# Second attention of a two-layer kernel: denominator, output and value units spread one or two to a batch, maxima spread after the next maxima, another order at the loop's end

## The reference, cut to what matters

```python
def _L1_attn_ref(x, gamma, w_qkv, w_out):
    ...
    xn = rms_norm(x, gamma)
    qkv = xn @ w_qkv
    ...
    q = q * scale
    sim = jnp.einsum('bhid,bhjd->bhij', q, k)
    attn = jax.nn.softmax(sim, axis=-1)
    out = jnp.einsum('bhij,bhjd->bhid', attn, v)
    out = jnp.transpose(out, (0, 2, 1, 3)).reshape(b, n, DIM_INNER)
    return out @ w_out

def _L1_ffn_ref(x, w1_w, w1_s, w2_w, w2_s, h1_w, h1_s, h2_w, h2_s, w3_w, w3_s):
    ...
    h = jax.nn.silu(_tlin(x, w1_w, w1_s)) * _tlin(x, w2_w, w2_s)
    h = jax.nn.gelu(_tlin(h, h1_w, h1_s), approximate=False)
    h = jax.nn.gelu(_tlin(h, h2_w, h2_s), approximate=False)
    return _tlin(h, w3_w, w3_s)
```

## Time and profile before

| what | value |
|---|---|
| median of 3 runs | 1216.94 us (1216.90 to 1218.71) |
| profiled execution | 1228.52 us, its span 1226.7 us |
| TensorE (PE) busy, matmuls | 1160.0 us, 95% |
| VectorE (DVE) busy | 848.9 us, 69% |
| GpSimd (POOL) busy | 783.7 us, 64% |
| ScalarE (ACT) busy | 597.9 us, 49% |
| mean granted TensorE clock | 0.978 of full speed |

### The profile page before, as it was taken

How to read it: one execution, slowest core, us unless ns; L and a number is a source line. 1 busy time by engine, 2 the same in 40 slices (tenths; PEclk the granted TensorE clock), 3 DMA queues, 4 the chain that set the end, 5 groups by cost and what they waited for, 6 DMA issues and landing times.

```text
span 1226.7 us, 21785 instructions
## 1 busy us (share of the span) xinstructions
PE 1160.0 (95%) x8892; PEld 738.6 (60%) x8892; DVE 848.9 (69%) x1078; ACT 597.9 (49%) x930; POOL 783.7 (64%) x503
## 2 busy tenths in 40 slices
PE   7999999998887989999999999999999999979997
PEld 6899999866654445454444454454454454447776
DVE  4665886565565577777787778777777777655543
ACT  1543344545564545554554555555555554634342
POOL 3565767753324568878878887888888888940000
PEclk9998999998997899999999999999999999989999
DMA  6000000020000020000000000000000000000000
GB/s 202 2 2 2 2 2 2 3 71 1 1 1 1 1 95 1 1 1 2 1 1 1 1 1 1 2 1 1 1 1 1 2 1 1 1 1 10 9 9 9
DMA packets 6978, 13.65 MB, mean 11 GB/s; under 512 B 1744, under 2 KB 4176, under 8 KB 6496
## 3 DMA queue, kind: packets, MB, share of 16 engines
q1 hardware_dynamic: 6096, 11.66, 2.8%
q10 hardware_dynamic: 784, 0.61, 0.3%
HBM read 11.22 MB, written 1.05 MB: 10 GB/s over the span
## 4 chain that ended last, share of the span: by engine, by line
PE 75%; DVE 13%; issue 4%; ACT 3%; POOL 3%; ACTq 1%; POOLq 0%; DVEq 0%
PE o_ps L1334 13%; PE mx_ps L1293 8%; PE ha_banks L494 6%; PE st_ps L1313 4%; PE st_ps L1316 4%; PE st_ps L1319 4%; DVE mx_part L1517 4%; PE bank L1695 3%; POOL acc L1612 3%; PE bank L1697 3%; PE bank L1696 3%; PE pj_ps L1245 2%; PE pj_ps L1264 2%; PE pj_ps L1256 2%; PE ha_banks L558 2%
## 5 line engine op out<-in xcount | busy, mean ns | idle before, releaser
L1612 POOL TENSOR_TENSOR acc<-acc,prob 128x1024 f32<-128x1024 f32 x192 | 467.1, 2433 | 89.7 <-ACT prob L1455 81.0
L1517 DVE TENSOR_REDUCE mx_part<-mx_ps 128x2 f32<-128x1024 f32 x251 | 303.8, 1210 | 112.4 <-PE mx_ps L1293 112.4
L1455 ACT ACTIVATE prob<-st_ps 128x1024 f32<-128x1024 f32 x256 | 248.6, 1022 | 198.0 <-PE st_ps L1319 194.6
L1334 PE MATMUL o_ps<-prob,v_cur 128*64 128x512 f32 x1024 | 247.7, 605 | 0.0
L1293 PE MATMUL mx_ps<-k_hi,q_hi 64*128 64x512 f32 x502 | 123.5, 489 | 9.0 <-DVE mx_part L1517 8.5
L1334 PEld LDWEIGHTS o_ps<-prob,v_cur 128*64 128x64 f32 x1024 | 66.6, 137 | 107.2 <-issue 103.4
L1293 PEld LDWEIGHTS mx_ps<-k_hi,q_hi 64*128 64x128 f32 x502 | 47.5, 186 | 134.8 <-DVE mx_part L1517 68.1
L1535 DVE RECIPROCAL rden<-rden 128x128 f32<-128x128 f32 x128 | 120.3, 942 | 9.3 <-ACT rden L1419 9.3
L1612 POOL TENSOR_TENSOR acc<-prob 128x1024 f32<-128x1024 f32 x32 | 76.0, 2374 | 46.2 <-PE pj_ps L1241 24.3
L1319 PE MATMUL st_ps<-q_hi,d_lo 64*128 64x512 f32 x512 | 102.0, 394 | 0.0
L752 POOL TENSOR_TENSOR ha_wide<-ha_pt,ha_own 128x512 f32<-128x512 f32 x64 | 73.8, 1184 | 8.6 <-ACT ha_pt L709 8.6
(11 more groups left out here) (362 smaller groups left out, 2222.5 us busy)
## 6 DMA issues: line engine op xcount, KB each, us to landing
h_w<-in_h SPq DMA_DIRECT2D x2, 1024.0 KB, 8.3
w_raw<-in_w SPq DMA_DIRECT2D x8, 192.0 KB, 3.5
x<-in_x SPq DMA_DIRECT2D x4, 256.0 KB, 7.3
head_wkv<-in_wkv SPq DMA_DIRECT2D x1, 1024.0 KB, 11.8
out<-fin SPq DMA_DIRECT2D x4, 256.0 KB, 2.2
m_w<-in_m SPq DMA_DIRECT2D x3, 256.0 KB, 2.9
sel_raw<-in_sel SPq DMA_DIRECT2D x1, 576.0 KB, 12.0
ha_head_pos<-in_pos ACTq DMA_DIRECT2D x2, 256.0 KB, 8.2
```

The source lines that it names most:

```text
L1334: mm = pe.matmul(o_ps[rows(h), :], v_cur[:, m % 2, j, rows(h)], prob[:, (16 * m + slot) % RING, h, :], start=(j == 0), stop=(j == KT - 1), ...
L1455: act.activation(prob[:, n % RING, :, :], st_ps[:, slot % 2, :, :], ACT.Exp, scale=SCALE).then_inc(s_exp, 1)
L1517: dve.reduce_max(mx_part[:, :, i, keys:keys + 1], maxima_banks(q, n), AX_X).then_inc(s_mxr, 1)
L1612: pool.tensor_tensor(total, old, new, ALU.add).then_inc(s_acc, 1)
```

## The change

It moves units between batches, moves the spread of maxima behind the second reduction, spreads reciprocals over other places, moves the 8 low parts of the last step from GpSimd to VectorE, and writes another order behind the loop.

```diff
-    INVERT = {(6, 0): (0, 0, 0), (6, 1): (0, 1, 0), (0, 0): (0, 2, -1), (1, 0): (0, 3, -1),
-              (2, 0): (1, 0, -1), (2, 1): (1, 1, -1), (4, 0): (1, 2, -1), (4, 1): (1, 3, -1)}
+    INVERT = {(0, 0): (0, 0, -1), (0, 1): (0, 1, -1), (1, 0): (0, 2, -1), (1, 1): (0, 3, -1),
+              (4, 1): (1, 0, -1), (5, 0): (1, 1, -1), (5, 1): (1, 2, -1), (6, 0): (1, 3, -1)}
...
-    BEFORE = (QK[0], QK[1], QK[2], ("tr", 1), QK[3], ("v", 0), ("out", 1), ("tr", 0))
-    AFTER = {1: ("den", 1), 2: ("out", 0), 5: ("den", 0), 6: ("v", 1)}
+    BEFORE = (QK[0], QK[1], QK[2], ("tr", 1), QK[3], ("v", 0), ("v", 1), ("tr", 0))
+    AFTER = {1: ("out", 1), 3: ("den", 1), 5: ("out", 0), 7: ("den", 0)}
...
-             ("den", 1): -1, ("out", 0): -1, ("out", 1): -1}
+             ("den", 1): -1, ("out", 0): -1, ("out", 1): -2}
...
         at_b = before(m, b)
+        if second:
+            vector_maxima(dve, *second)
         if at_b and at_b[1][0] == "tr":
             vector_spread_max(dve, *at_b)
-        if second:
-            vector_maxima(dve, *second)
         if at_b and at_b[1][0] == "qk":
             vector_low(dve, *at_b)
-        if at_b and at_b[1][0] == "out":
-            vector_add_out(dve, *at_b)
         vector_invert(dve, m, b, 1)
-        if b == 1 and m >= 1:
+        if b == 3 and m >= 1:
             vector_normalize(dve, m - 1, 0)
-        if b == 5 and m >= 1:
+        if b == 6 and m >= 1:
             vector_normalize(dve, m - 1, 1)
...
+    def vector_split(dve, i):
+        n, t = tiles[i]
+        dve.wait_ge(s_hi_w, i + 1)
+        dve.tensor_tensor(w_lo[n][:, t, :], raw[n][:, t, :], w_hi[n][t][:, :].bitcast(F32), ALU.subtract).then_inc(s_lo_v, 1)
...
                 end.tensor_first(pe, 0, 2)
-                t2.tensor(pe, STEPS, 2)
                 end.tensor_first(pe, 0, 3)
                 end.tensor_hidden(pe, 0, 1, 0)
+                t2.tensor(pe, STEPS, 3)
                 end.tensor_hidden(pe, 0, 1, 1)
-                t2.tensor(pe, STEPS, 6)
+                t2.tensor(pe, STEPS, 5)
+                end.tensor_hidden(pe, 0, 1, 2)
+                end.tensor_hidden(pe, 0, 1, 3)
+                end.tensor_hidden(pe, 0, 2, 0)
+                t2.tensor(pe, STEPS + 1, 1)
...
                 for m in range(STEPS):
                     for b in range(BATCHES):
                         t2.vector(dve, m, b)
+                        if m == END:
+                            end.vector_split(dve, split_at(m, b))
                 end.vector_x(dve, 0)
...
-                        if slot % 2 and split_at(m, slot // 2) is not None:
+                        if m < END and slot % 2 and split_at(m, slot // 2) is not None:
                             end.gpsimd_split(pool, split_at(m, slot // 2))
```

More of the change, by code:

```diff
@@ L1160, in second_attention @@
     turns = [(0, QK[3]), (0, QK[2]), (0, ("v", 0)), (0, ("v", 1)), (0, ("tr", 0))]
-    turns += [u for m in range(STEPS + 1) for b in range(BATCHES)
+    turns += [u for m in range(STEPS + 2) for b in range(BATCHES)
               for u in [before(m, b), after(m, b)] + norm_at(m, b) if u]
@@ L1648, in last_network @@
     bank = at.banks(*((f"bank{i}", [P, CH]) for i in range(BANKS + 1)))
-    s_raw, s_hi_w, s_lo_w = at.sem("s_raw2"), at.sem("s_hi_w"), at.sem("s_lo_w")
+    s_raw, s_hi_w, s_lo_w, s_lo_v = at.sem("s_raw2"), at.sem("s_hi_w"), at.sem("s_lo_w"), at.sem("s_lo_v")
     s_full = [at.sem(f"s_full{i}") for i in range(BANKS)]
@@ L1716, in bank_free, with split @@
             pe.wait_ge(s_sg, k * HT + m + 1)
+    def split(pe, w):
+        if cut_by[w] <= EARLY:
+            pe.wait_ge(s_lo_w, cut_by[w])
+        else:
+            pe.wait_ge(s_lo_v, cut_by[w] - EARLY)
     def tensor_first(pe, k, m):
@@ L1723, in tensor_first @@
             if k == 0 and m == 0:
-                pe.wait_ge(s_lo_w, cut_by[w])
+                split(pe, w)
             bank_free(pe, b, n)
@@ L1743, in tensor_last @@
                 if k == 0:
-                    pe.wait_ge(s_lo_w, cut_by["m3"])
+                    split(pe, "m3")
                     pe.wait_ge(t2.s_out, 2 * STEPS)
@@ L1863, in last_network @@
     s.tensor_first, s.tensor_hidden, s.tensor_last = tensor_first, tensor_hidden, tensor_last
-    s.gpsimd_split, s.scalar_split, s.scalar_first, s.scalar_hidden, s.scalar_last = (
-        gpsimd_split, scalar_split, scalar_first, scalar_hidden, scalar_last)
+    s.vector_split, s.gpsimd_split, s.scalar_split, s.scalar_first, s.scalar_hidden, s.scalar_last = (
+        vector_split, gpsimd_split, scalar_split, scalar_first, scalar_hidden, scalar_last)
     s.vector_x, s.vector_first, s.vector_hidden, s.vector_last = vector_x, vector_first, vector_hidden, vector_last
@@ L1983, in _ @@
                         for m in range(HT):
-                            if (k, layer) != (0, 1) or m >= 2:
+                            if (k, layer) != (0, 1) and (k, layer, m) != (0, 2, 0):
                                 end.tensor_hidden(pe, k, layer, m)
@@ L2016, in _ @@
                 t2.scalar(act, STEPS, 0)
-                end.scalar_first(act, 0, 0)
-                end.scalar_first(act, 0, 1)
-                t2.scalar(act, STEPS, 1)
-                end.scalar_first(act, 0, 2)
-                end.scalar_first(act, 0, 3)
+                for m in range(HT):
+                    end.scalar_first(act, 0, m)
+                end.scalar_hidden(act, 0, 1, 0)
+                t2.scalar(act, STEPS, 3)
                 for k in range(CHUNKS):
@@ L2028, in _ @@
                         for m in range(HT):
-                            end.scalar_hidden(act, k, layer, m)
+                            if (k, layer, m) != (0, 1, 0):
+                                end.scalar_hidden(act, k, layer, m)
                 end.scalar_last(act, CHUNKS - 1)
@@ L2055, in _ @@
                 end.vector_first(dve, 0, 0)
-                t2.vector(dve, STEPS, 1)
                 end.vector_first(dve, 0, 1)
@@ L2059, in _ @@
                 end.vector_first(dve, 0, 2)
+                end.vector_first(dve, 0, 3)
+                t2.vector(dve, STEPS, 1)
                 t2.vector(dve, STEPS, 3)
+                end.vector_x(dve, 1)
+                end.vector_hidden(dve, 0, 1, 0)
                 t2.vector(dve, STEPS, 4)
+                end.vector_hidden(dve, 0, 1, 1)
                 t2.vector(dve, STEPS, 5)
-                end.vector_first(dve, 0, 3)
+                end.vector_hidden(dve, 0, 1, 2)
                 t2.vector(dve, STEPS, 6)
+                end.vector_hidden(dve, 0, 1, 3)
+                end.vector_hidden(dve, 0, 2, 0)
+                t2.vector(dve, STEPS + 1, 2)
                 for k in range(CHUNKS):
@@ L2069, in _ @@
                             end.vector_first(dve, k, m)
-                    if k + 1 < CHUNKS:
+                    if k and k + 1 < CHUNKS:
                         end.vector_x(dve, k + 1)
@@ L2073, in _ @@
                         for m in range(HT):
-                            end.vector_hidden(dve, k, layer, m)
+                            if (k, layer) != (0, 1) and (k, layer, m) != (0, 2, 0):
+                                end.vector_hidden(dve, k, layer, m)
                 end.vector_last(dve, CHUNKS - 1)
```

## The result

| | before | after |
|---|---|---|
| first comparison: median (lowest to highest) | 1216.97 us (1216.90 to 1218.71), 4 runs | 1232.28 us (1230.05 to 1234.53), 4 runs |
| profiled execution | 1228.52 us, span 1226.7 | 1234.53 us, span 1232.7 |

The ratio of after to before is 1.0122, interval 1.0102 to 1.0143: the change makes the kernel slower. The forecast of 1224 us had the sign, but the result lies 0.28 us above its range of 1211 to 1232. Medians lie 15.3 us apart, the two profiled executions 6.0 us.

The account below looks back on a forecast made before the run. TensorE's in-order list was taken as the bound. Terms +10.9 - 2.6 + 0.4 + 2.2 - 3.6 = +7.3 us took the profiled 1228.5 to 1235.8; carrying over the 11.6 us above the median gave 1224, range 1211 to 1232.

Parts of the forecast that it names:

- Steady steps: Steps 2 to 14: removed and added waits sum to +0.84 us a step, +10.9 over 13 steps.
- Removed: b3 and b7 of a steady step: the wait behind `q_max` goes, 0.29 us each, together -0.58.
- In b1: Steady step: a reciprocal delays the first reduction, for which the second maxima product waits, +0.40 us.
- In b6: Steady step: the value unit waits for the addition of the `out` unit in the same bank, +1.02 us.
- Step 1: b2 of step 1: `xr_lo` comes earlier and the 2.24 us wait goes; -2.6 us with the steady +0.84.
- Step 0: b7 of step 0: a unit of the norm waits behind the denominator unit, +0.4 us.
- Last step and `x_lo`: Last step: low parts on VectorE delay reductions, +2.2 us; behind the loop TensorE waits 5.0 us for `x_lo`.
- Behind the first network product: Behind the loop: the 6.12 us wait goes, the 1.90 us wait falls to 0.8, the second slow stretch goes (-1.4).
- Rival 1: Behind the loop: `x_lo` is ready at 1080.3, 4.4 us less wait and 1.4 less slow clock, 1218.4 us; chance 0.15.
- Rival 2: b6 and b1: new waits don't reach the end of a step, which is 0.58 us shorter; 1204.4 us, chance 0.14.
- Rival 3: b6: normalised outputs miss GpSimd, 0.9 us more in each of 14 steps, 1237 us; chance 0.08.
- Rival 4: Steady steps: the clock falls at each 1.0 us wait, 1.4 us 14 times, 1244 us; chance 0.05.

Follow-up runs that it names:

- e4: Kernel before with one edit, the spread of maxima moved behind the second reduction: 1215.96 us, ratio 0.9963 to before.
- first pair: First profiled executions of the kernel before and the changed kernel: 1228.52 and 1234.53 us.
- e3: Changed kernel with the addition ahead of the reciprocal in b6 and no reciprocal ahead of b1's first reduction: 1218.88 us, ratio 0.9986 to before.
- after again: Changed kernel repeated unchanged on chip 5: 1226.79 us, ratio 1.0054 to before.
- e5: Changed kernel with x_hi and x_lo made earlier, behind b6 of the last step: 1219.08 us in a single run.
- second pair: Both kernels repeated unchanged on chip 5 and profiled: before 1220.75 us (12 runs), after 1226.79 us.
- e1: Changed kernel with only the addition of the out unit put ahead of the reciprocal in b6: 1224.49 us in a single run.
- e8: Changed kernel with the 8 low parts of the last step back on GpSimd: 1227.21 us in a single run.

## Why the prediction was right or wrong

**Steady steps, right within 0.1 us a step.** Removed: -0.55 (e4) against -0.58. In b1 +0.35 (2.17 less 1.82) against +0.40. In b6 the value unit of after starts 1.40 us behind the second maxima product. In before the unit in that place starts 0.43 behind it (at 686.49):

```profile
686.06 0.50 PE L1293 MATMUL mx_ps<-k_hi,q_hi 64*128 64x512 f32 x2
```

That is +0.97 against +1.02, as the unit followed the start of the addition by 0.68 us where I had 0.73. Together +0.77; the measured period rose by 0.89 (43.38 to 44.27). The 0.1 between them is in what I put at nothing, the moved units: from e4 to after b3 and b7 grow by 0.75 and 0.91 us, and b2 and b6 give back 0.69 and, the 0.97 apart, 0.86. Errors of both signs made +10.9 into +11.5.

**Step 1, right.** `xr_lo` fell to 0.76 us and the wait of 2.24 went. How much that is worth depends on the half clock behind it: -3.9 in the first pair, -2.8 in the second. Both hold some 0.9 us for the `out` unit that step 1 has less, which I had left out; with it my sum would have been -3.5. Step 0: +0.6 to +0.8 against +0.4.

**Last step and `x_lo`, right in kind.** 1.43 + 0.61 against 2.2, and 4.41 against 5.0. ScalarE's last cut is at 1085.39, 1.1 us before TensorE is there (1090.91 less 4.41), as the prediction had it (0.9 to 1.2). Behind it come a low part of 2.05 us, a cast of 0.42 and `x_lo` of 2.71: two of the three operations were long where I took all three as waiting for an addition. (The lower bound of this wait should read 0.5 and not 0.6 us: 1080.3 less 1079.8.)

The Trainium skill says in "SBUF — State Buffer", section "Who interferes with whom", that a VectorE instruction with two SBUF inputs contends with a GpSimd instruction that reads SBUF. The trace agrees, and it was worth 2 us on an instruction: `x_lo` 2.71 us under GpSimd's additions, `xr_lo` 2.79 or 0.68 by the moment at which it starts, `o_n` 0.69 to 2.24 in e3. How long one takes depends on how far the addition under way has got: of the low parts in the rows above one took 0.78 us and one 2.05.

**Behind the first network product, -7.4 and -8.3 in the two pairs against -8.6, right in kind.** The 6.12 us are gone, 0.28 and 0.34 (for `act13lo`) are left of the waits where I had left 0.8, and the second slow stretch is gone: behind 1096.32 after has no product at half clock. The first slow stretch stays, as forecast, but its length varies: 12 products take 5.41 us in after and 4.54 in after again, and 0.9 us is also what the two pairs differ by. The `out` unit that I left out in step 1 is paid here. One reading of mine is off: 7 products in 2.40 us are not 0.34 each, since the window cuts some of them; from start to start they are 0.43 apart against 0.23, which is the 0.2 that the sum used.

**The rivals.** Rival 1 (`x_lo` early) is what e5 builds: the change doesn't do it. Its two terms, 4.4 and 1.4 us less, came out as 4.5 and 1.5 there. Rival 2 fell: both waits reach the end of the step. Rival 3 fell for the change but not as a mechanism; e3 uncovers it. Rival 4 fell: behind the 0.91 us of b6 the clock stays at 1.00 in the steady steps.

**The step that failed** is the last of the total: the profiled execution "is 11.6 us above the median of 1216.94; I carry the difference over unchanged: 1224". The sum of parts was +7.3 us, traces of the second pair give +7.4, and the forecast of 1235.8 for the profiled execution met 1234.53. But the distance from a profiled execution to the median is not fixed. In the change it was 2.3 us (1234.53 less 1232.28), and in the repeats -0.6 (before), 0.8 (after) and 0.3 (after, third time). A profiled execution is one draw from the spread of its program: of before, 1216 to 1229 us over all sets, which three runs that agreed within 1.8 us hid. With 2.3 in the place of 11.6 the forecast would have been 1233.5. That 1235.8 came so near has some luck in it, as both first profiles drew a slow step 0 (57.83 and 58.65 us).

**Open:** why the first comparison has 15.3 us between its medians where the stretches of the traces add up to 7.4. Its four runs of before (1216.90 to 1218.71) lie at the low edge of what that program did elsewhere. The chip or the occasion has a part: on chip 7 the fastest of 11 runs of before took 1219.62 us, and the medians of before were 1219.88, 1222.82 and 1223.81 on chips 5, 0 and 7. So whether the first ratio, 1.0122, is chance, or whether that chip favours one kernel, is not shown. Open is also what decides in which execution step 0 runs at full clock. In 13 profiles of ten kernels step 0 takes 57.8 to 58.7 us in nine and 53.6 to 56.0 in four, with and without the change, and the way to step 0 varies as much, from 366.3 to 372.7. I tried nothing that steers either.

## What to carry to other kernels

Where one engine's list is the bound, price a reordering by the one result that each wait hangs on, and look for what stands ahead of that result on the engine that makes it: here a reciprocal of 0.86 us ahead of a reduction cost 0.35 us in each of 13 steps, and one ahead of an addition 0.80. A wait that is removed can uncover the next one (`o_n` ahead of b7 in e1 and e3), so look one step behind it. Work moved to another engine also moves when that engine is done: with the low parts back on GpSimd its additions ran longer, and VectorE's `act01lo` met them (e8). When a profile lies away from a median, ask for the spread before building on either.

## What the runs showed of the hardware

The granted clock around the start of the second attention differs between executions of one program: step 0 took 57.83 us with the clock at 0.89 to 0.92 and 53.62 at 1.00. A wait of 2.24 us in step 1 was followed by a unit of 1.69 us in one execution, and one of 2.25 by a unit of 1.08 in the other.

An operation of VectorE with two inputs in SBUF had to wait for GpSimd's addition under way. In the steady steps, and in step 1, those whose own time is 0.68 us ended 2.9 us behind the start of that addition, wherever they began within it: `xr_lo` of before, 0.13 us behind it, took 2.79; `o_n` in b6 of after, 1.33 us behind it (687.60 to an addition from 686.27), took 1.58; the `o_n` of 2.09 us in e3 began 0.84 us behind one. So `o_n` took 1.59 and 2.09 us in steps of one loop with one period, in the same place, and 0.69 behind the loop, where GpSimd did nothing. A cover that holds in one step fell short in another. A cast with one input took 0.42 us in after and 2.60 in e5.
